# A neighbour sum on one core: TensorE multiplies a constant tile twelve times behind each item

## The reference, cut to what matters

```
h = feats * rsqrt(deg_out)[:, None]
m = segment_sum(h[src], dst, num_segments=n) * rsqrt(deg_in)[:, None]
gc = m @ W_gc + b_gc
```

## Time and profile before

| | us |
|---|---|
| Median of 3 runs | 8009.14 (7997.09 to 8013.13) |
| The profiled execution's own time | 7960.64 |
| Its span, first to last instruction | 7958.6 |
| PE busy / PEld / DVE / ACT / POOL | 4644.0 / 3297.6 / 3630.5 / 2267.6 / 3134.6 |
| PE's mean granted clock, share of 2.4 GHz | 0.749 |

### The profile page before, as it was taken

How to read it: one execution, slowest core, us unless ns; L and a number is a source line. 1 busy time by engine, 2 the same in 40 slices (tenths; PEclk the granted TensorE clock), 3 DMA queues, 4 the chain that set the end, 5 groups by cost and what they waited for, 6 DMA issues and landing times. The chain is left out here.

```text
span 7958.6 us, 97165 instructions
## 1 busy us (share of the span) xinstructions
PE 4644.0 (58%) x25691; PEld 3297.6 (41%) x25691; DVE 3630.5 (46%) x7669; ACT 2267.6 (28%) x7764; POOL 3134.6 (39%) x3162
## 2 busy tenths in 40 slices
PE   1698576677776404454445532886265666666664
PEld 1465344455455302233223321775122555555542
DVE  8111566666664341121112220111323888888875
ACT  0233355555553210000001210221011555444550
POOL 0320566666660027767763002001102666565640
PEclk9999677778778756666666556998566888888885
DMA  3333666666662223333334013883214666666662
GB/s 109 97 124 130 194 197 198 199 199 202 198 194 71 57 70 95 94 90 94 94 91 72 26 28 127 265 262 91 58 61 127 205 206 209 202 203 202 205 155 77
DMA packets 603761, 1110.04 MB, mean 139 GB/s; under 512 B 157032, under 2 KB 416238, under 8 KB 599843
## 3 DMA queue, kind: packets, MB, share of 16 engines
q0 software_dynamic: 204144, 617.42, 27.6%
q1 hardware_dynamic: 399216, 488.05, 19.0%
HBM read 983.67 MB, written 208.59 MB: 150 GB/s over the span
## 5 line engine op out<-in xcount | busy, mean ns | idle before, releaser
L714 POOL DMA_INDIRECT l3e_kv<-t_table,k_recs x912 | 971.7, 1065 | 670.6 <-ACT l3e_vw L991 370.4
L714 POOL DMA_INDIRECT l0e_kv<-t_table,k_recs x912 | 984.3, 1079 | 635.4 <-ACT l0e_vw L991 372.4
L1371 PE MATMUL l2e_pA<-l2e_row,l2e_oh 128*128 128x257 f32 x1824 | 644.5, 468 | 914.9 <-issue 625.6
L1325 POOL DMA_INDIRECT l2e_row<-t_table,l2e_idx x912 | 899.2, 986 | 391.8 <-issue 270.7
L1371 PEld LDWEIGHTS l2e_pA<-l2e_row,l2e_oh 128*128 128x128 f32 x1824 | 409.5, 229 | 1149.8 <-issue 1107.2
L948 PE MATMUL l0e_pA<-l0e_vw,l0e_ohf 128*128 128x260 f32 x1824 | 652.8, 505 | 205.3 <-ACT l0e_vw L991 132.3
L991 ACT ACTIVATE l3e_vw<-l3e_kv,l3e_w 128x64 f32<-128x64 f32 x2736 | 679.8, 334 | 0.1
L991 ACT ACTIVATE l0e_vw<-l0e_kv,l0e_w 128x64 f32<-128x64 f32 x2736 | 679.7, 334 | 0.0
L900 PE MATMUL l3e_pQE<-l3e_qb,l3e_ohT 128*128 128x256 bf16 x2736 | 427.4, 318 | 402.3 <-issue 375.1
L1350 DVE SCALAR_TENSOR_TENSOR l2e_acc<-l2e_acc,k_itf,l2e_pA 128x257 f32<-128x257 f32 x228 | 109.6, 481 | 1058.8 <-issue 935.6
L948 PEld LDWEIGHTS l0e_pA<-l0e_vw,l0e_ohf 128*128 128x128 f32 x1824 | 428.1, 248 | 346.8 <-ACT l0e_vw L991 157.0
(11 more groups left out here) (452 smaller groups left out, 7553.8 us busy)
## 6 DMA issues: line engine op xcount, KB each, us to landing
exp_w<-in_L_gnn_w SPq DMA_DIRECT2D x224, 512.0 KB
t_table<-l0n_tab SPq DMA_DIRECT2D x26, 2048.0 KB, 6.8
l0e_qb<-t_q SPq DMA_DIRECT2D x228, 192.0 KB
l3e_qb<-t_q SPq DMA_DIRECT2D x228, 192.0 KB
t_agg<-l0e_acc SPq DMA_DIRECT2D x228, 130.0 KB
t_agg<-l3e_acc SPq DMA_DIRECT2D x228, 130.0 KB
l0e_drow<-t_drow SPq DMA_DIRECT2D x57, 512.0 KB
l3e_drow<-t_drow SPq DMA_DIRECT2D x57, 512.0 KB
```

The costliest lines, as they stand in the source:

```text
L714: pool.indirect_dma_start(kv[:, n % SK, g, :], None, table[:, :], bass.IndirectOffsetOnAxis(ap=K["recs"][:, n, g, ridx:ridx + 1], axis=0)) ...
L1325: pool.indirect_dma_start(row[:, s, g, 0:D], None, table[:, :], bass.IndirectOffsetOnAxis(ap=idx[:, i, g:g + 1], axis=0)).then_inc(row_rea ...
L1371: last = pe.matmul(pA[s % SB][:, 0:W], oh[:, s, g, :], row[:, s, g, :], start=(g == 0), stop=(g == G - 1))
```

## The change

Behind each item's 4 sums PE does 12 more matmuls: the unit matrix in bf16 (`identb`, made by the first stage) as weights, times a tile `wide` of 128x512 bf16 that POOL fills with zeros at the stage's start. Each writes a whole bank of 128x512, `pW`, that nobody reads. They wait for nothing, raise nothing and stand behind the sum that raises `a_ps`. As `pW` takes one of the 8 banks, the accumulators go from 8 to 7, and the bank of an item is now chosen by i mod 7 on both engines.

```diff
         W = D + 1
-        SB = 8
+        SB = 7
+        FILL = 12
...
+        wide = S.sb("wide", [P, 512], BF16)
         pA = [S.ps(f"pA{j}", [P, 512]) for j in range(SB)]
+        pW = S.ps("pW", [P, 512])
...
             pool.memset(row[:, :, :, D:W], 1.0)
+            pool.memset(wide[:, :], 0.0)
...
-                dve.scalar_tensor_tensor(out=acc[:, s, :], in0=acc[:, before, :], scalar=K["itf"][:, i, 1:2], in1=pA[s % SB][:, 0:W],
+                dve.scalar_tensor_tensor(out=acc[:, s, :], in0=acc[:, before, :], scalar=K["itf"][:, i, 1:2], in1=pA[i % SB][:, 0:W],
...
                 for g in range(G):
-                    last = pe.matmul(pA[s % SB][:, 0:W], oh[:, s, g, :], row[:, s, g, :], start=(g == 0), stop=(g == G - 1))
+                    last = pe.matmul(pA[i % SB][:, 0:W], oh[:, s, g, :], row[:, s, g, :], start=(g == 0), stop=(g == G - 1))
                 last.then_inc(a_ps[s], 1)
+                for u in range(FILL):
+                    pe.matmul(pW[:, :], K["identb"][:, :], wide[:, :], start=True, stop=True)
```

## The result

The changed kernel takes 8078.32 us (median of 4 runs, 8066.36 to 8088.59) against 8003.11 us for the kernel before (4 runs, 7970.19 to 8013.13): +75 us, ratio 1.0097 with a 95% interval of 1.0072 to 1.0123. The forecast was 8080 us, +73 us on the stage.

What follows compares the result with a forecast made beforehand. The stage was taken as bound by POOL's indirect DMAs (1140 us) plus waits for a delayed PE. 228 x 6.0 + 7 = 1375 us against 1302, +73 us on the 8009 us median: predicted 8080 us, range 7880 to 8270.

Steps and rivals of the forecast that it cites:

- rival A: Added matmuls keep PE quick, thin work being the cause; POOL's waits go, stage 1181 us, -121 us; chance 0.24.
- The quick item: PE's undelayed item with 12 added matmuls: 1.92 + 2.9 = 4.8 us (3.4 to 4.8), under POOL's 5.0 us.
- The bank at 0 to 2 us: One accumulator bank fewer lets PE run 7 items ahead of DVE's reads, not 8; cost nothing to 2 us.
- The mean item: Average item in the stage with PE's delays included: 6.0 us, chosen between 5.7 and 6.95 us.
- all 228 items at POOL's pace: Stage as 228 x 6.0 = 1368 us, with 7 us for first rows and end: 1375 us.
- its own backlog of near 16 items: PE at best 4.8 us against POOL's 5.0, so its backlog stays near 16 items, tying POOL to PE.
- The scaling of the delay by pairs (8 to 20): PE's delay per matmul-and-load pair kept: 8 pairs' 1.0 and 2.3 us become 2.4 and 5.8; wholly slow item 56 us.
- "POOL waits for PE" as what bounds the stage before: Above POOL's 1140 us floor, mostly 120 us in 28 waits for slots that PE had not freed.
- B: Rival: POOL's finer stops keep the delay from building up; stage 1215 to 1307 us, -87 to +5 us; chance 0.12.
- C: Rival: short stops don't reset PE, delay stays deep; items 8 us or more, stage 1824 us, +520 us; chance 0.06.
- D: Rival: no delay in unprofiled runs, PE's 4.8 us under POOL's 5.0 us; no change, 8009 us; chance 0.10.

Runs made afterwards that it cites:

- e4: Kernel before, gather replaced by plain SP loads of consecutive rows, plus a DVE reduction behind each add; stage 1107 us, program time not comparable.
- e11: Changed kernel with POOL clearing a scratch tile and draining after every 16 indirect DMAs; ratio 1.0077 to the kernel before, stage 1378 us.
- e1: Changed kernel without its 12 added matmuls, seven banks kept; 7953.76 us against 7950.61 for the kernel before, ratio 1.0008.
- e6: Changed kernel with 6 added matmuls in place of 12; ratio 1.0037 to the kernel before, stage 1354 us.
- e2: Changed kernel with its 12 added matmuls cut from 512 to 16 columns; ratio 1.0052 to the kernel before, stage 1344 us.
- e3: Kernel before, POOL held at most 4 items ahead of PE in place of 16; ratio 1.0005, stage 1307 us.
- e5: Changed kernel, POOL held at most 4 items ahead of PE in place of 16; ratio 1.0032 to the kernel before, stage 1341 us.
- e8: Kernel before, each indirect DMA moving half a row (128 floats); stage 1329 us, program time not comparable.
- e7: Kernel before, POOL clearing a scratch tile and draining after every 16 indirect DMAs; ratio 1.0067, stage 1379 us.
- e9: Kernel before, POOL draining after every 16 indirect DMAs, no clearing; ratio 1.0046, stage 1345 us.
- e12: Kernel before, POOL clearing a scratch tile and draining after every 32 indirect DMAs; ratio 1.0019, stage 1322 us.
- e10: Kernel before, POOL draining after every 32 indirect DMAs, no clearing; ratio 1.0015, stage 1318 us.

## Why the prediction was right, and which of its steps were not

**The direction and the reason against rival A: shown.** PE's delay is not cured by work on PE. It comes with POOL's indirect DMAs (e4: none without them) and lands on the added matmuls themselves at a clock of 0.82 to 1.0 (the rows at 3417 to 3421). The Trainium skill (TensorE: Matmul & The Clock Gate, "Why this matters for your kernels") is right here on the clock, 0.65 to 0.87, and the stage was 79 us longer all the same, because PE's clock bounded nothing.

**The quick item: 4.33 us, forecast 4.8.** The added matmul of 512 columns starts each 0.216 us, forecast 0.24 (range 0.12 to 0.245); the Trainium skill (same page, "Back-to-back issue gap") gives 216 ns for a single matmul's gap, and the trace agrees. Its lower figure of about 131 ns for a sustained stream of such pairs of load and matmul is not seen here. That this is under POOL's 5.0 us, and so covered where PE isn't delayed, e11 shows. The bank at 0 to 2 us: e1, not distinguishable from nothing.

**The mean item: 6.03 us, forecast 6.0.** The mean distance of first records over all 228 items is 5.69 us before and 6.03 after. The size is right, its composition is not, and 6.0 us was a choice between 5.7 and 6.95 us, so that the total came out at 8080 us for 8078 is in part luck.

**The step that failed: all 228 items at POOL's pace.** The forecast put every item at 6.0 us, which gives 1368 us, and 7 us for the start and the end. But its own backlog of near 16 items means that POOL is done some 14 items early, and that these 14 go at the quick pace. Measured, 214 items go in POOL's run of 1320 us, 6.17 us each, and 14 at 4.33 us in a tail of 61 us. The delayed items took 36 us more than 6.0 us each would have, the tail's items 23 us less. From the forecast's own numbers it would have been 214 x 6.0 + 14 x 4.8 = 1351 us in all, 33 us too low: two errors met. By place the 79 us are +30 us of POOL's run, +47 us of tail and +1 us at the start; the forecast saw stops of POOL all along and no tail. POOL's stops went from 121.5 us in 28 pieces to 159.7 us in 49, all for PE's sums: more and in more pieces, as forecast, but by 38 us, not by the 73 us of the whole. (One reading of the prediction is off by 1 us: POOL's instructions are 33 us longer than 0.95 us each, not 34.)

**The scaling of the delay by pairs (8 to 20): borne out for the deepest item, not as an average.** The longest item, from its first to its last load, is 18.2 us with 8 pairs, 36.4 with 14 (e6), and 43.8 (e2) and 42.0 with 20; between adds it was 46 us (forecast 56). But the late time within items fell from 700 to 301 us in the stage. With 6 added matmuls it is 536 (e6), and with 12 of 16 columns 638 (e2). So the sum doesn't grow with the count of pairs; it was smaller the longer PE computed. The semaphores say the same: adds start 19.3 us behind the last record in the mean before, 4.3 us in the changed kernel. Nor do DVE's adds come evenly 6 us apart: 11.7 us of nothing, then 1.0 and 4.9 us.

**"POOL waits for PE" as what bounds the stage before: right as far as the waits go, open behind them.** All of POOL's stops before, in the changed kernel and in e1, e2, e3, e5, e6 and e8 are waits for a semaphore of PE that is late. e3 doesn't refute that; it only moves the delay out of the records. Stops that POOL makes itself take the waits away (e7, e9, e12), but they cost as much or more. POOL's run, less the 1140 us of 912 DMAs 1.25 us apart, was 150 us before, 149 in e3, 154 in e1 and in e8, 163 to 170 in e10, e2, e12 and e6, and 180 to 224 in the others: never under 149 us, though POOL was stopped by PE in few long pieces, in many short ones, or by itself. That is 1.41 us for a DMA at best. The drains are long themselves: one takes longer behind 32 DMAs than behind 16, and a memset of 1.8 us ahead of it shortens it by only 0.5 us (32; e10, e12) or 1.1 us (16; e9, e7). That the indirect DMAs leave something behind that must be worked off, for which drains wait and which holds up PE's semaphores too, is argued from this, not shown. What it is stays open, and so does whether PE computes late or only reports late; e8 says only that it isn't the bytes. No kernel here ran the gather on POOL unbroken to its floor, and none with the gather beat the kernel before.

**The +30 us of POOL's run** come from the stops: 38 us more of them, every one a wait for PE's late sums. With a lead of 4 the added matmuls raise the stops likewise, from 140 us (e3) to 164 us (e5). By how much an added matmul delays a sum under POOL's stream was not taken further.

**Rivals A, B and C** are out by the stage's 1384 us (1181, 1215 to 1307, 1824). **D** is out by the ratio's interval.

## What to carry to other kernels

An engine that idles half the time still holds a backlog when it is late in bursts, and work added to it is paid for where the producer has ended: the items ahead times the item's new length, here 14 x 4.33 = 61 us where 14 us had been, six tenths of the cost. So when adding "free" work, price the drain of the queue at the end, and shorten the lead if it is long. Read when an engine is done from what its semaphore lets go, not from its records alone: in e3 no record of PE was late, and yet its sums were reported up to 16 us behind them, and POOL waited for that. When a producer waits for a consumer, remove that wait once by another way before you count on winning it: here the stops that POOL made itself cost as much as the waits. A higher TensorE clock is worth something only where the matmuls' length is on the path.

## What the runs showed of the hardware that was not expected

- POOL's indirect DMAs of 128 rows start 1.25 us apart in bursts of tens, but here no run of 912 went faster than 1.41 us each (1289 us in e3), and with rows of 512 B in place of 1 KB it was 1.42 us (e8).
- A drain on POOL behind such DMAs leaves a gap of 3.2 us after 16 and 3.9 us after 32 of them, and still 2.1 us (16) and 3.4 us (32) with a memset of 1.82 us ahead of it.
- Beside POOL's stream of indirect DMAs PE's semaphores come late behind the records that raise them, by up to 78 us in the kernel before, and in the deeper cases the records start late too, by steps of about 0.7 us. Without those DMAs (e4) all 228 semaphores came 0.01 us behind the record.
- Holding POOL to 4 items ahead (e3), or 28 stops of 5.4 us (e12), took away the late starts but not the late semaphores (up to 16.2 and 20.7 us) and changed the stage's time by +2 and +16 us. Stops behind each 16 DMAs (e7, e9) brought the semaphores to at most 3.2 us behind.
